# Shared-key attention: three banks of scores with one maximum each, and four banks of transposed scores in one ring

## The reference, cut to what matters

```python
def _L2_xattn_ref(q, k, v):           # q = layernorm(x), k = v = ctx_512
    B, S, E = q.shape
    H, KV = (32, 8)
    D = E // H
    G = H // KV
    qh = q.reshape(B, S, KV, G, D).transpose(0, 2, 3, 1, 4)
    kh = k.reshape(B, S, KV, D).transpose(0, 2, 1, 3)
    vh = v.reshape(B, S, KV, D).transpose(0, 2, 1, 3)
    scores = jnp.einsum('bkgsd,bktd->bkgst', qh, kh) / math.sqrt(D)
    weights = jax.nn.softmax(scores, axis=-1)
    out = jnp.einsum('bkgst,bktd->bkgsd', weights, vh)
    return out.transpose(0, 3, 1, 2, 4).reshape(B, S, E)
```

## Time and profile before

| | |
|---|---|
| median of 3 runs | 3703.59 us (3701.0 to 3709.85) |
| the profiled execution: its time, its span | 3709.56 us, 3707.7 us |
| PE busy | 3084.9 us, 83% of the span |
| DVE busy | 2243.4 us, 61% |
| ACT busy | 1801.0 us, 49% |
| mean granted clock of PE | 0.908 of full |
| maxima of scores (line 1702, both attentions) | x768, 620.4 us busy |
| exponentials (line 1683) | x1024, 528.6 us busy |
| first and last maximum of layer 2, of layer 3 | about 1674 to 2030 us, 2887 to 3242 us |

### The profile page before, as it was taken

The page is one execution under the profiler, slowest core; times in us unless marked ns, Lnnn a source line. Parts: engine busy times, 40 slices in busy tenths (PEclk is TensorE's granted clock), DMA queues, the critical chain, the costliest instruction groups (busy, mean ns, idle before and its releaser), DMA issues. The chain is left out here.

```text
span 3707.7 us, 55886 instructions
## 1 busy us (share of the span) xinstructions
PE 3084.9 (83%) x15750; PEld 2116.6 (57%) x15750; DVE 2243.4 (61%) x3802; ACT 1801.0 (49%) x3122; POOL 559.7 (15%) x1150
## 2 busy tenths in 40 slices
PE   3329999879872799928998699899898899979998
PEld 2117777645461688823333388788786333338886
DVE  6974445456443333358998444566556899936655
ACT  5643333535430455525777533566533577753443
POOL 2430000024422000040111040122111011100000
PEclk7659999879985899967999799999999799979999
DMA  4424444866361433343321262576643432102333
GB/s 139 143 96 136 136 137 136 306 166 149 90 233 40 127 107 108 104 149 95 80 62 36 77 209 93 176 244 235 214 139 95 127 79 62 42 21 91 94 98 113
DMA packets 241080, 461.87 MB, mean 125 GB/s; under 512 B 57444, under 2 KB 73956, under 8 KB 240402
## 3 DMA queue, kind: packets, MB, share of 16 engines
q1 hardware_dynamic: 207602, 343.64, 30.5%
q0 software_dynamic: 22480, 96.23, 7.7%
q10 hardware_dynamic: 10864, 20.45, 1.5%
HBM read 343.78 MB, written 113.77 MB: 123 GB/s over the span
## 5 line engine op out<-in xcount | busy, mean ns | idle before, releaser
L1702 DVE TENSOR_REDUCE at_maxima<-psum 128x1 f32<-128x512 f32 (+1 forms) x768 | 620.4, 859 | 36.0 <-PE psum L1610 30.2
L1683 ACT ACTIVATE at_probs<-psum 128x512 f32<-128x512 f32 x1024 | 528.6, 604 | 208.2 <-PE psum L1626 208.2
L1626 PE MATMUL psum<-at_qT,at_kT 50*128 50x512 f32 x1024 | 375.6, 456 | 71.0 <-ACT at_probs L1683 54.3
L601 PE MATMUL psum<-f_xT_hi,ffn_w_hi 128*128 x1024 | 406.5, 397 | 10.4 <-DVE f_xT_lo L313 2.8
L601 PE MATMUL psum<-f_xT_lo,ffn_w_hi 128*128 x1024 | 406.0, 397 | 0.0
L1610 PE MATMUL psum<-at_kT,at_qT 48*128 48x512 f32 x1024 | 387.0, 482 | 12.1 <-DVE at_maxima L1702 9.7
L1626 PEld LDWEIGHTS psum<-at_qT,at_kT 50*128 50x128 f32 x1024 | 171.0, 190 | 364.3 <-ACT at_probs L1683 243.8
L1639 PE MATMUL psum<-at_probs,at_vals 128*32 128x512 f32 x2048 | 281.2, 622 | 0.0
L393 PE MATMUL psum<-ident,n_normed 128*128 128x128 f32 x512 | 102.6, 369 | 202.1 <-ACT n_normed L356 159.5
L618 PE MATMUL psum<-ffn_w_hi,ffn_hid_hi 128*128 128x512 f32 x768 | 269.2, 391 | 1.3 <-ACT ffn_hid_hi L667 1.3
L490 ACT ACTIVATE ffn_w_hi<-ffn_w_raw 128x512 fp32r<-128x512 f32 x262 | 161.7, 633 | 156.2 <-PE psum L623 101.1
(11 more groups left out here) (381 smaller groups left out, 6701.5 us busy)
## 6 DMA issues: line engine op xcount, KB each, us to landing
ffn_w_raw<-in_stream SPq DMA_DIRECT2D x262, 256.0 KB, 2.7
ffn_w_hi<-quantized SPq DMA_DIRECT2D x66, 512.0 KB, 3.6
ffn_w_hi<-quantized SPq DMA_DIRECT2D x65, 256.0 KB, 3.2
at_qT<-q_hi SPq DMA_DIRECT2D x256, 64.0 KB, 2.3
ffn2a_w_raw<-in_shared2a SPq DMA_DIRECT2D x26, 512.0 KB
qz_raw<-in_stream SPq DMA_DIRECT2D x17, 768.0 KB, 4.2
quantized<-qz_quant POOLq DMA_DIRECT2D x16, 768.0 KB, 3.5
gathered<-zeros SPq DMA_DIRECT2D x1, 12288.0 KB
```

Of the source, the lines that this page charges most:

```text
L601: mm = pe.matmul(hid_ps[h][s][0:n, :], wt[s][:, w], xt[:, c, bass.ds(b * S, S)], start=(c == 0 and i == 0), stop=(c == DC - 1 and i == len ...
L1626: pe.matmul(scoreT[turn_of(n)][:, :], kT[r][half(h % 2, USED + 2), t * P:(t + 1) * P], qT[r][half(h % 2, USED + 2), h // 2, :], start=True ...
L1683: act.activation(probs[n % RING][:, :], scoreT[turn_of(n)][:, :], ACT.Exp, scale=factor).then_inc(exped, 1)
L1702: dve.tensor_reduce(maxima[g % 2][:, h:h + banks, t], scores, AX.X, ALU.max).then_inc(maxed, 1)
```

## The change

Banks 0 to 2 now hold scores and banks 3 to 6 transposed scores (SCORES, TURNS = 3, 4). Every tile has its own maximum over one bank: 16 instructions of 128 x 512 elements for a group instead of 12. Scores go round the three banks without a restart at a group (`score_of`), so the score of tile n waits for the maximum of tile n - 3, for every n. Transposed scores and `turn_results` share one ring of four banks that runs on through all slots with 17 uses a slot (`use_of`, `turn_of`); `wait_for_bank` waits for the use four before: the exponential of tile n - 4, or of n - 3 where the turned results lie between, or `finished` where that use was the turned results (n = 11). `turn_results` waits for the exponential of n = 4 of its slot instead of n = 5. The two semaphore increments that offset `exped` are gone.

```diff
-    SETS = [(n, 2 if n % 4 == 0 else 1) for n in range(PAIRS) if n % 4 != 1]
...
-    TURNS = 3
+    SCORES, TURNS = 3, 4
...
-        score, scoreT, res = room.banks[0:4], room.banks[4:4 + TURNS], room.banks[7]
-        turn = room.tiles(4 + (RES + 1) % TURNS)
+        score, scoreT, res = room.banks[0:SCORES], room.banks[SCORES:SCORES + TURNS], room.banks[7]
...
+        def score_of(g, n):
+
+            return score[(PAIRS * g + n) % SCORES]
+
+        def use_of(g, n):
+
+            return (PAIRS + 1) * g + (n if n <= RES else n + 1)
+
+        def turn_of(g):
+
+            return (PAIRS + 1) * (g + 1) + RES + 1
+
+        def turn_tiles(g):
+
+            return room.tiles(SCORES + turn_of(g) % TURNS)
+
+        def wait_for_bank(pe, use):
+
+            g, n = divmod(use - TURNS, PAIRS + 1)
+            if n == RES + 1:
+                if g > 0:
+                    pe.wait_ge(finished, g + 1)
+            elif g >= 0:
+                pe.wait_ge(exped, PAIRS * g + (n if n <= RES else n - 1) + 1)
...
-                if n % 4 != 1:
-                    pe.wait_ge(maxed, len(SETS) * g + set_of(n) + 1)
-                mm = pe.matmul(score[n % 4][:, :], qT[r][half(par, USED), jj, t * P:(t + 1) * P], kT[r][half(par, USED), :],
-                               start=True, stop=True)
-                if n % 4 != 0:
-                    mm.then_inc(scored, 1)
+                pe.wait_ge(maxed, PAIRS * g + n + 1)
+                pe.matmul(score_of(g, n)[:, :], qT[r][half(par, USED), jj, t * P:(t + 1) * P], kT[r][half(par, USED), :],
+                          start=True, stop=True).then_inc(scored, 1)
...
-                if n < 2:
-                    pe.wait_ge(exped, PAIRS * g + n + 1)
-                elif n > 2:
-                    pe.wait_ge(exped, PAIRS * g + (n + 1 if RES < n < RES + TURNS else n))
-                if n == RES + TURNS and g > 0:
-                    pe.wait_ge(finished, g + 1)
+                wait_for_bank(pe, use_of(g, n))
...
                     if n == RES and s > 0:
                         pe.wait_ge(res_moved, s)
-                        pe.wait_ge(exped, PAIRS * s + n + 1)
-                        turn_results()
+                        wait_for_bank(pe, turn_of(s - 1))
+                        turn_results(s - 1)
...
-            act.sem_inc(exped, 2)
...
-            dve.sem_inc(maxed, 3)
+            dve.sem_inc(maxed, SCORES)
...
-            def max_set(g, m):
-                n, banks = SETS[m]
+            def maximum(g, n):
                 jj, par, t = head_tile(n)
                 h = 2 * jj + 1 - par
-                dve.wait_ge(scored, len(SETS) * g + m + 1)
-                scores = room.psum[:, 512 * (n % 4):512 * (n % 4 + banks)].rearrange("p (h s) -> p h s", h=banks)
-                dve.tensor_reduce(maxima[g % 2][:, h:h + banks, t], scores, AX.X, ALU.max).then_inc(maxed, 1)
+                dve.wait_ge(scored, PAIRS * g + n + 1)
+                dve.tensor_reduce(maxima[g % 2][:, h:h + 1, t], score_of(g, n)[:, :], AX.X, ALU.max).then_inc(maxed, 1)
...
-                    if m == set_of(RES) and s > 0:
+                    if m == RES and s > 0:
                         finish(s - 1)
```

More of the change, by code:

```diff
@@ L1619, in scores_T @@
                     pe.wait_ge(put[r], PUTS * DMA * (g // SLOTS + 1))
-                if n < 2:
-                    pe.wait_ge(exped, PAIRS * g + n + 1)
-                elif n > 2:
-                    pe.wait_ge(exped, PAIRS * g + (n + 1 if RES < n < RES + TURNS else n))
-                if n == RES + TURNS and g > 0:
-                    pe.wait_ge(finished, g + 1)
-                pe.matmul(scoreT[turn_of(n)][:, :], kT[r][half(h % 2, USED + 2), t * P:(t + 1) * P], qT[r][half(h % 2, USED + 2), h // 2, :],
+                wait_for_bank(pe, use_of(g, n))
+                pe.matmul(scoreT[use_of(g, n) % TURNS][:, :], kT[r][half(h % 2, USED + 2), t * P:(t + 1) * P], qT[r][half(h % 2, USED + 2), h // 2, :],
                           start=True, stop=True).then_inc(scoredT, 1)
@@ L1637, in results, with turn_results @@
                     n = t * H + h
-                    pe.wait_ge(exped, 2 + PAIRS * g + n + 1)
+                    pe.wait_ge(exped, PAIRS * g + n + 1)
                     pe.matmul(res[h * OW:(h + 1) * OW, :], vals[g % 2][:, t, :], probs[n % RING][:, :],
                               start=(t == 0), stop=(t == TB - 1), tile_position=(0, h * OW), skip_group_check=True).then_inc(valued, 1)
-            def turn_results():
+            def turn_results(g):
+                turn = turn_tiles(g)
                 for t in range(TB):
@@ L1662, in _ @@
                         pe.wait_ge(res_moved, s)
-                        pe.wait_ge(exped, PAIRS * s + n + 1)
-                        turn_results()
+                        wait_for_bank(pe, turn_of(s - 1))
+                        turn_results(s - 1)
             results(GROUPS - 1, TB - 1)
             pe.wait_ge(res_moved, GROUPS)
-            turn_results()
+            turn_results(GROUPS - 1)
         @block.scalar
         def _(act):
-            act.sem_inc(exped, 2)
             def move_res(g):
@@ L1682, in _ @@
                     act.wait_ge(valued, PAIRS * s + n + 1)
-                    act.activation(probs[n % RING][:, :], scoreT[turn_of(n)][:, :], ACT.Exp, scale=factor).then_inc(exped, 1)
+                    act.activation(probs[n % RING][:, :], scoreT[use_of(s, n) % TURNS][:, :], ACT.Exp, scale=factor).then_inc(exped, 1)
                     if n == MOVE and s > 0:
@@ L1719, in _ @@
             for g in range(LEAD):
-                for m in range(len(SETS)):
-                    max_set(g, m)
+                for m in range(PAIRS):
+                    maximum(g, m)
                     if m == 0 and g > 0:
@@ L1724, in _ @@
             for s in range(GROUPS):
-                for m in range(len(SETS)):
+                for m in range(PAIRS):
                     if s + LEAD < GROUPS:
-                        max_set(s + LEAD, m)
+                        maximum(s + LEAD, m)
                     if m == 0 and s + PUT < GROUPS:
                         turn_maxima(s + PUT)
-                    if m == set_of(RES) and s > 0:
+                    if m == RES and s > 0:
                         finish(s - 1)
```

2 lines of the change are left out of this document (1 added, 1 removed).

## The result

| | before | changed |
|---|---|---|
| median of 20 runs | 3702.41 us (3696.64 to 3720.91) | 3717.04 us (3709.68 to 3719.94) |
| ratio to before | | 1.0033, 95% interval 1.0023 to 1.0042 |
| profiled execution: its time, its span | 3709.56, 3707.7 us | 3709.68, 3707.9 us |
| a slot in the steady part of layer 2 | 11.22 us | 11.70 us |
| a slot of the last three of layer 2 | 11.18 us | 9.03 us |

The changed kernel is slower by 0.33%, some 12 us (9 to 16 by the interval; the two medians lie 14.6 us apart). The two profiled executions happen to be equally long, so the total of a single execution says nothing here: the changed one reached its first maximum of layer 2 at 1664.61 us and the one before at 1674.15, and the change touches nothing ahead of that. The slots say it: there the two traces differ by much more than their scatter.

What follows compares the result with a forecast made beforehand. PE's loop with ACT through three transposed-score banks was taken as the bound, replaced by one through DVE. Per call +0.5 + 14.6 + 0.9 - 6.5 = +9.5 us, two calls +19: 3723 us, range 3703 to 3742.

Steps and rivals of the forecast that it cites:

- The loop: PE and DVE through three banks of scores: 2.73 us a quarter, in three quarters of a slot.
- The parts of the loop: Score to its maximum 0.57 us, maximum 0.68, release of PE 0.05 (at most 0.15), then 0.43 and 1.00.
- The quarter with the finish: From pair 7 through turn_results, RECIPROCAL, TENSOR_TENSOR and tile 8's maximum until pair 11 may go: 3.55 us.
- Lead-in: Three groups where DVE alone sets the pace: 9.7 us a group against 9.40, +0.9 us a call.
- The last slots: Last three slots, without scores: ACT's floor of 8.3 us and a hole, about 9.0; -6.5 us a call.
- The single maxima: Split of the double maxima: four more instructions a group cost DVE 0.2 us, not entering the loop whole.
- The first: Rival: DVE at full pace if tile 4's score is ready in time; slot 10.4 us, about 3647; chance 0.08.
- the second: Rival: no difference, the quarter with `finish` stays near 3.2 us; slot 11.4, total 3704; chance 0.14.
- the third: Rival: a tile's two matmuls come apart, 0.23 us into each quarter's loop; +52 us, 3775; chance 0.06.
- the fourth: Rival: exponentials still hold PE, so the last slots gain nothing; +13 us, 3736; chance 0.04.
- The total: Two calls of +9.5 us each, +19 us; the forecast itself, +8 to +42 us, has chance 0.68.
- slot 0: First slot, four plain quarters at +0.1 us each: +0.5 us a call.

Runs made afterwards that it cites:

- the run with four banks of scores: Changed kernel with four banks of scores, three of transposed scores, still one maximum per bank: 3716.64 us against 3720.25 for the kernel before, ratio 0.9992.
- the second chip: Changed kernel as it stands, measured again on another chip: 3733.22 us against 3728.18 for the kernel before, ratio 1.0019 (1.0004 to 1.0033).
- the fourth run: Kernel before, each maximum taken over half of its scores: 3711.85 us in a single execution, against 3720.25.
- the third: Changed kernel, each maximum taken over the first 256 of 512 scores: 3677.0 us in a single execution, against 3720.25 for the kernel before.

## Why the prediction was right, point by point

- **The loop.** Forecast 2.73 us in three quarters, measured 2.74 to 2.75 (1823.76 to 1826.51), with PE waiting for the maximum of the first tile behind the results. Both half-maximum runs carry it: 0.26 us less in a maximum takes 1.06 us from this kernel's slot and nothing from the one of before.
- **The parts of the loop.** The score to its maximum 0.57 (1825.19 to 1825.76), which had not been seen alone, and the release 0.05 were right; the other end of the release, 0.15, which made the upper bound of +42 us, does not show behind these maxima (1829.26 + 0.68 to 1829.99). DVE's stall behind each `results`, forecast as some 0.4, shows as an idle time of 0.17 to 0.26; it is what is left over in the loop and no term of its sum. The stated range ends at 3742, 4 us short of its own bound (3704 + 42).
- **The quarter with the finish.** Forecast 3.55, measured 3.48: mostly because the maximum behind the TENSOR_TENSOR starts 0.35 after it (1828.91 to 1829.26) and not 0.40 as the double did. Less the 0.01 that each plain quarter is longer, that is the 0.04 by which the slot came out under 11.74.
- **Lead-in.** Forecast +0.3 us a group, measured +0.39 (9.79 for 9.40).
- **The last slots.** Forecast 9.0 from ACT's floor and a hole; measured 9.03, with ACT's holes of 0.24 to 0.26 where I had put one of 0.6. The sum came out and the one hole did not, so that it came out this closely is in part luck.
- **The single maxima.** The rows of before put them at 0.2 us of DVE a slot, hidden in DVE's waits; the run with four banks of scores shows 11.20 for 11.22. They cost something only where DVE is the bound, and that is the lead-in, in which it works with next to no gap: there a group with its four more instructions took 0.39 us more, a small wait of the transpose included. The 125 ns an instruction of the Trainium skill (Perfetto Trace Analysis, Optimizing Scalar/DVE Operations) would make an estimated 0.5 us of that, and its advice on larger operations is tied to an engine that is saturated. The lead-in lies between the 0.2 of the rows and the 0.5; the slots, where the measured cost is none, show the condition.
- **Rivals.** The first fell on the point named for it: the score of tile 4 comes too late, and DVE has a gap behind every block of results. In the second, the quarter with the finish did not stay at 3.2. In the third, transposed score and score do come apart (1826.00 and 1826.51), but only where PE waits anyway. In the fourth, the last slots did gain.

**The total** was forecast as +19 us, and came out as +12 (9 to 16), and less on the second chip: the direction is right, and about a third of the size did not come. In layer 2 the slots give 27 x 0.48 = 13.0 us (forecast 14.6), less 0.8, 2.1, 2.1 and 0.3 in the last four distances between RECIPROCALs (5.3, forecast 6.5): +7.7 us a call. Two terms that follow the clock of PE were not in the sum, or only within its bounds.

*The lead-in and slot 0* were forecast as +1.4 us together. From the first maximum to the first RECIPROCAL the kernel before took 48.16 us in layer 2 and 45.15 in layer 3, the changed one 47.01 and 50.03: 1.1 less in one call and 4.9 more in the other. The granted clock is half of full (1.2 of 2.4 GHz) in nearly the whole lead-in (0.50 from 1684 to 1694 us in the kernel before), where PE waits for DVE's maxima, and rises to full at some moment of slot 0: 43 and 35 us behind the first maximum before, 37 and 45 us in the changed kernel. The windows of slot 0, of before and then of the changed kernel (us, busy of PE, PEld, DVE, ACT, POOL, the granted clock, DMA, GB/s):

```profile
1702.00:1722.00 20.00, 19.62 (x90) 7.60 (x87) 14.98 (x21) 12.42 (x24) 1.31 (x6) 0.61 0.52 163
2916.00:2933.00 17.00, 16.20 (x91) 6.36 (x89) 14.92 (x22) 12.30 (x24) 1.11 (x6) 0.81 0.55 177
```

```profile
1693.00:1712.00 19.00, 18.65 (x96) 9.22 (x97) 16.16 (x30) 13.46 (x25) 1.30 (x6) 0.79 0.49 164
2913.00:2935.00 22.00, 21.88 (x96) 10.43 (x96) 16.13 (x30) 13.47 (x26) 1.30 (x6) 0.62 0.46 152
```

In either kernel the call with the lower clock there takes 3.0 us longer. So slot 0 can hide or double the few us of its own term, whichever kernel runs.

*The last slots* have such a case too. In layer 3 of the kernel before they were not 11.18 us long:

```profile
3247.86 0.26 DVE L1713 RECIPROCAL at_inv<-psum 128x16 f32<-128x16 f32 x1 [4.62 <-PE psum L1644]
...
3260.59 0.26 DVE L1713 RECIPROCAL at_inv<-psum 128x16 f32<-128x16 f32 x1 [12.02 <-PE psum L1644]
...
3274.42 0.26 DVE L1713 RECIPROCAL at_inv<-psum 128x16 f32<-128x16 f32 x1 [13.12 <-PE psum L1644]
...
3285.71 0.26 DVE L1713 RECIPROCAL at_inv<-psum 128x16 f32<-128x16 f32 x1 [10.58 <-PE psum L1644]
```

12.73, 13.83 and 11.29 us, where layer 2 has 11.18, 11.18 and 7.57: 7.9 us more. The granted clock was 0.67 there. The window of before, and then two of the changed kernel:

```profile
3254.00:3285.00 31.00, 27.39 (x109) 7.97 (x109) 1.36 (x4) 17.73 (x35) 1.70 (x3) 0.67 0.00 1
```

```profile
2036.00:2058.00 22.00, 21.72 (x129) 7.58 (x128) 2.04 (x6) 20.76 (x43) 2.43 (x4) 1.00 0.01 2
3254.00:3285.00 31.00, 30.41 (x176) 10.12 (x174) 4.55 (x11) 27.73 (x56) 3.11 (x7) 1.00 0.01 2
```

In those slots of layer 2 PE had been 18.01 us busy in 22 (82%) at full clock and is 21.72 in 22 now; in the changed kernel's last slots the clock stayed at full in both calls. The Trainium skill (TensorE: Matmul & The Clock Gate, Part 1: The HAM clock gate) says that the gate sets the clock by how busy PE has recently been. The traces agree in part: the busier slots never lost their clock, but of the less busy ones, alike in their work, some did and some did not. A fall inside the last slots was in three of ten calls of profiled executions with last slots of 11.1 to 11.2 us, in none of the four with 10.6 and in none of the ten with 9.0 to 9.3. One execution a kernel doesn't settle how often it comes, so that the kernel before loses time to it more often than the changed one is a reading, and not shown.

Together, from the first maximum to the last RECIPROCAL, the two profiled executions hold 392.15 and 398.17 us before and 398.67 and 401.65 after: +6.5 and +3.5, 10 us in all, which lies in the measured 9 to 16. In layer 3 the +4.9 ahead of the first RECIPROCAL and the 7.9 at the end go against each other, and one slot of the kernel before, 12.32 us, holds a wait of its own for the maxima's way through DRAM. So the sum of the slots was sound, and how the remaining difference of some us to the +19 spreads over many executions stays open.

## What to carry to other kernels

When PE, in order, feeds two consumers through small rings of banks, don't ask which engine is fullest but walk the loop: the first tile behind a long block of PE work, its consumer's whole latency, the tile that waits for that bank, and the block again. A bank moved from one ring to the other only changes whose latency stands in the loop, and a busy share of 93% does not say that an engine is in it. What shortens such a loop is the order: put other PE work into the stretch where PE waits, and change how many tiles lie between two blocks of results, rather than buy banks.

## What the runs showed of the hardware that was not expected

- Shortening DVE's work in the lead-in (both half-maximum runs) turned into a wait for the transfers that bring the maxima back through DRAM. The idle times of PE's transposed scores that end with such a transfer, matmuls and weight loads added up over both calls, are 28.6 us (8 times) in the fourth run against 3.8 us (3 times) in the kernel before, and 37.5 us (15 times) in the third against none in the changed kernel. At the present pace the lead of three groups is just about enough.
- A maximum over one bank of PSUM that follows a TENSOR_TENSOR starts 0.35 us behind it (1828.91 to 1829.26), one over two banks 0.40 (1834.78 to 1835.18).
